# Chunked and channel attention on one core: values ahead of mask and scores on TensorE, low half ahead of the maximum on VectorE

## The reference, cut to what matters

```
scores = einsum('bnqhd,bnkhd->bnhqk', qh, kh) * scale
scores = scores + where(km > 0, 0.0, NEG)
attn = softmax(scores, axis=-1)
out = einsum('bnhqk,bnkhd->bnqhd', attn, vh).reshape(N, T, C)
out = (out @ W_out.T + b_out).transpose(0, 2, 1) * masks + x_of_layer_0
```

## Time and profile before

| what | value |
|---|---|
| median of 3 runs | 1578.93 us (1578.62 to 1580.92) |
| profiled execution | 1581.6 us, span 1579.8 us |
| busy: PE, PEld, DVE, ACT, POOL | 98%, 83%, 85%, 63%, 29% |
| mean granted TensorE clock | 0.991 of full speed |
| period of a sample, from the start of L803 in sample 8 to that in sample 9 | 822.36 to 918.01 us |

### The profile page before, as it was taken

One profiled execution on the slowest core, in us unless ns is written; L12 is line 12 of the kernel. 1 busy time (PEld: TensorE's weight loads), 2 busy tenths in 40 slices (PEclk: granted clock), 3 DMA queues, 4 the chain that ended last, 5 costly groups with the idle time before them and its releaser, 6 DMA issues.

```text
span 1579.8 us, 53821 instructions
## 1 busy us (share of the span) xinstructions
PE 1541.7 (98%) x23816; PEld 1307.8 (83%) x23816; DVE 1339.2 (85%) x2024; ACT 993.3 (63%) x1796; POOL 463.2 (29%) x292
## 2 busy tenths in 40 slices
PE   7999999999999999999999999999999999999994
PEld 6888888888888888888888888888888888888873
DVE  4778889898898888989888898888988889898886
ACT  5557665666656667576576656666566675765753
POOL 0114233142331414124142331423314142241422
PEclk9999999999999999999999999999999999999996
DMA  6132341423323242241523314233242423415021
GB/s 233 60 95 88 96 127 43 148 82 115 109 74 123 69 142 82 94 128 43 150 87 103 122 42 148 82 116 107 68 129 69 141 82 95 128 43 153 31 74 62
DMA packets 96328, 157.22 MB, mean 100 GB/s; under 512 B 5344, under 2 KB 38240, under 8 KB 95968
## 3 DMA queue, kind: packets, MB, share of 16 engines
q1 hardware_dynamic: 96096, 153.78, 31.2%
HBM read 120.20 MB, written 33.55 MB: 97 GB/s over the span
## 4 chain that ended last, share of the span: by engine, by line
PE 97%; DVE 1%; ACT 1%; issue 0%; DMA 0%; POOL 0%; DVEq 0%; SPq 0%; POOLq 0%; ACTq 0%
PE pj_ps L283 46%; PE l_ps L283 12%; PE w_ps L318 7%; PE s_ps L307 7%; PE l_ps L392 7%; PE w_ps L336 6%; PE s_ps L296 3%; PE l_ps L410 2%; PE l_ps L430 2%; PE l_ps L418 1%; PE l_ps L424 1%; PE l_ps L412 1%; PE l_ps L433 1%; DMA y_raw<-in_ctx 0%; PE l_ps L400 0%
## 5 line engine op out<-in xcount | busy, mean ns | idle before, releaser
L946 POOL TENSOR_TENSOR prob<-prob,row_inv 128x1024 f32<-128x1024 f32 x128 | 262.3, 2049 | 927.1 <-DVE row_inv L740 927.1
L596 ACT CAST att_hi<-w_ps 128x256 fp32r<-128x256 f32 x256 | 82.8, 376 | 249.5 <-PE w_ps L336 243.7
L283 PE MATMUL pj_ps<-y_hi,w_hi 128*128 128x512 f32 x512 | 209.0, 408 | 9.3 <-DVE y_lo L705 9.3
L283 PE MATMUL pj_ps<-y_lo,w_hi 128*128 128x512 f32 x512 | 203.3, 397 | 0.0
L283 PE MATMUL pj_ps<-y_hi,w_lo 128*128 128x512 f32 x512 | 203.2, 397 | 0.0
L735 DVE TENSOR_REDUCE row_sum<-prob 128x16 f32<-128x1024 f32 x128 | 155.0, 1211 | 52.3 <-ACT prob L578 52.3
L723 DVE TENSOR_REDUCE row_max<-s_ps 128x16 f32<-128x1024 f32 x128 | 155.9, 1218 | 20.1 <-PE s_ps L307 17.6
L963 POOL TENSOR_TENSOR o_sb<-o_sb,u_sb 128x1024 f32<-128x1024 f32 x63 | 164.7, 2625 | 6.7 <-ACT o_sb L586 6.7
L573 ACT COPY prob_t<-w_ps 128x512 f32<-128x512 f32 x256 | 149.9, 586 | 19.7 <-PE w_ps L318 16.8
L709 DVE TENSOR_TENSOR yt_hl<-yt_raw,yt_hl 128x1024 fp32r<-128x1024 f32 x64 | 119.7, 1870 | 43.0 <-ACT yt_hl L545 41.0
L730 DVE TENSOR_TENSOR prob<-s_ps,row_max 128x1024 f32<-128x1024 f32 x128 | 155.5, 1215 | 0.1
(11 more groups left out here) (110 smaller groups left out, 3581.9 us busy)
## 6 DMA issues: line engine op xcount, KB each, us to landing
y_raw<-in_ctx SPq DMA_DIRECT2D x64, 512.0 KB, 4.9
yt_raw<-in_ctx_t SPq DMA_DIRECT2D x64, 512.0 KB, 4.7
x_raw<-in_x SPq DMA_DIRECT2D x64, 512.0 KB, 5.1
out_z<-o_sb SPq DMA_DIRECT2D x64, 512.0 KB, 3.6
mask_b<-in_mask SPq DMA_DIRECT2D x64, 256.0 KB, 4.0
u_sb<-in_w SPq DMA_DIRECT2D x2, 512.0 KB, 5.0
w_sb<-in_w SPq DMA_DIRECT2D x1, 1024.0 KB, 10.7
cst<-in_consts SPq DMA_DIRECT2D x1, 512.0 KB, 6.9
```

Of the source, the lines that this page charges most:

```text
L283: last = mm(dst, lhs, rhs, start=i == 0, stop=i == len(todo) - 1)
L946: nc.gpsimd.tensor_tensor(cut, cut, row_inv[:, u % 2, :].unsqueeze(2).to_broadcast([P, 2 * HEADS, CHUNK]), ALU.mult).then_inc(probs_done, 1)
```

## The change

On PE, in each even step, the 32 matmuls of `values` move from behind the mask and the scores to ahead of them. Their wait (`values_ready`) stood ahead of the scores already. On DVE, in each even step, the two subtractions of `att_low` move from behind `top` to ahead of it, with their wait for `att_hi_done`. Nothing is added or taken away, and what stands ahead of and behind these three things is as it was. The work behind the last step is not touched.

```
                     if e == 0:
                         if not (first and u < LAG):
                             values_ready(n, u - LAG)
+                            values(n, u - LAG)
                         scores(n, u)
-                        if not (first and u < LAG):
-                            values(n, u - LAG)
...
                     if e == 0:
-                        top(n, u)
                         if not (first and u < LAG):
                             att_low(n, u - LAG)
+                        top(n, u)
                         if s == 0 and not first:
                             group_deviation(n - 1)
                         shift(n, u)
```

## The result

The changed kernel takes 1592.61 us (median of 4 runs, 1589.19 to 1594.30) against 1579.56 (4 runs, 1578.62 to 1580.92): ratio 1.0079, 95% interval 1.0060 to 1.0099. The profiled execution took 1594.3 us, its span is 1592.5. The change makes the kernel 13 us slower.

A forecast was written before the change was run, and what follows sets the result against it. PE, busy 98% of the span, was taken to bound the kernel. 15 samples x 0.86 = 12.9, less 0.3, plus 0.1, gave +12.7 us: median 1591.6, own range 1588 to 1596, wider range 1579.5 to 1606 (0.81).

The forecast's parts named there:

- The hidden wait: PE's transposes in steps 6 and 10 wait 0.15 us for `att_lo`; removing it wins 32 x 0.15 = 4.8 us.
- The seams: PE's switches between kinds of matmul: taken as 0, with bounds of -10 to +10 us over 126 steps.
- The rival of the seams: PE's matmul switches at their bounds, with the main effect: 1581.6 or 1601.6 us; chance 0.09.
- Step 6: Transposes win 0.15 us; DVE's shift comes 0.7 us late, covered by the copy L803, which ends with POOL's join.
- The rival that the copy takes 2.02 us anywhere: L803 on DVE ends 0.7 us late, making step 10's shift 1.6 late: 24 us, time 1603; chance 0.12.
- Step 10: Transposes win 0.15 us; DVE waits for `att_hi` with `top` queued, so the shift is 0.86 us late, and `o_bias` too.
- The wait: PE waits 1.16 us for `o_bias` ahead of `layer0_output` in step 12, in 15 samples.
- The size: Net loss of 0.86 us a sample (bounds 0.74 to 1.01), in 15 samples: 12.9 us.
- no slack at all between step 10 and step 12: DVE, busy 10.58 of 10.68 us up to `o_bias`, passes any delay of step 10's shift on to PE.
- The sum: Whole kernel: 12.9 - 0.3 (first sample) + 0.1 (very end) = +12.7 us, median to 1591.6.
- The clock: A 1.16 us wait lowers TensorE's clock, 1.7 us more in 15 samples: time 1617; chance 0.07.
- The faster case: Early `att_hi` in step 10, or slack up to `o_bias`, leaves only the 4.8 us gains: 1574.1; chance 0.12.

The follow-up runs named there:

- the whole hold gone: Changed kernel with all of `split_y` (ACT's rounding of ctx) moved behind `copy_att` of the next step: 1576.23 us, ratio 0.9980 to the kernel before.
- all but step 10: Kernel before with the new order on PE and DVE in every even step except step 10, which keeps the old: 1579.33 us, ratio 0.9994.
- PE's half: Kernel before with only PE's order changed (values ahead of mask and scores), DVE still taking the maximum first: 1594.71 us, ratio 1.0098.

## Why the prediction was right, point by point

**What bounds.** The hidden wait of 0.15 us in steps 6 and 10 was real and went in both (PE takes 0.18 and 0.19 us less from step 6 to step 8 and from step 10 to step 12); with a repair the change gains, by the medians 2.9 us with `split_y` moved, 4.0 with the scaling moved and 5.3 with both, against 4.8 forecast.

**The seams.** 0 was taken. Values behind projection 0.32, mask behind values 0.79 from start to start, as the projection stood before. The rival of the seams falls.

**Step 6.** The low half was forecast 0.42 us sooner than needed and came 0.43 sooner (it ends at 825.91, the transposes start at 826.48 and need 0.14). The copy was forecast to end 0.15 behind POOL's join; measured 0.16. The rival that the copy takes 2.02 us anywhere falls. The Trainium skill's rule of the locked port pair (SBUF — State Buffer, Who interferes with whom) agrees: the copy started later, took 1.13 us, and ended with the join again.

**Step 10.** The shift was forecast to end 1.01 late against the step's start, measured 1.01 (5.73 against 4.72). The prediction says that the scores are ready 0.8 us sooner; ahead of the maximum it is 1.14 by its own rows, measured 1.13; no term of the sum uses it. The overlap lost between maximum and shift is in the rows: the shift starts 0.04 behind the maximum's end (847.23 + 1.21 = 848.44, 848.48). The Trainium skill's statement that a semaphore between two DVE instructions costs nothing extra (VectorE: DVE Perf Modes, The DRAIN you can't avoid), which it makes of a row of equal copies, does not hold for this pair: 0.04 behind the end, where instructions that don't wait for the one just ahead start 0.08 ahead of its end.

**The wait.** 1.16 us forecast, 1.16 measured.

**The size.** Forecast +0.86 a sample, measured +0.79: the two gains are 0.18 and 0.19 us, not 0.15, the part from step 12 to step 14 is 1.18 longer, and that behind it 0.03 shorter. The term that was mis-sized is the count: 14 samples, not 15. In the last sample ACT rounds nothing in step 9, and I carried the middle sample's row over. The rows of it after, step 10:

```profile
1523.60 0.65 ACT L595 CAST att_hi<-w_ps 128x256 fp32r<-128x256 f32 x2
...
1524.28 0.76 DVE L746 TENSOR_TENSOR att_lo<-w_ps,att_hi 128x256 fp32r<-128x256 f32 x2 [1.08 <-ACT att_hi L595]
...
1529.19 0.75 DVE L751 SCALAR_TENSOR_TENSOR u_sb<-pj_ps,c,mask_b 128x512 f32<-128x512 f32 x1 [0.85 <-PE pj_ps L283]
...
1537.03 0.47 PE L283 MATMUL l_ps<-x_hi,m_hi 128*128 128x512 f32 x1
```

`att_hi` comes 1 us sooner and no wait is marked in step 12, while DVE has 0.85 us to spare in step 11. This is no clean control for the hold, though. The low half of ctx (L704, 1.21 us in sample 8) is missing on DVE too, and before the change DVE was idle there for 1.03 us ahead of the same instruction, enough to swallow a shift that comes 1.01 late. So the prediction's "no slack at all between step 10 and step 12" holds for the middle samples only. The constant 0.26 us behind `o_bias` in sample 15 says that `o_bias` releases PE (2.08 us behind the start of step 12, where 2.06 is the least), but not that a later shift would delay it: DVE itself waits for PE on the way. The proof of the middle samples is the wait itself, and its going when the scaling moved.

**The sum.** From the start of sample 1 to that of sample 15 there are 14 periods, 0.79 us longer each: +11.1. The part ahead of sample 1 is 0.7 shorter and that from the start of sample 15 to the end 0.3, with the two gains of the first and of the last sample in them. That is +10.1, where the forecast had 12.7. The rest was not forecast: some samples are longer than the median, mostly those with the stops told of in the last section, by 5.0 us in all after and by 2.4 before, +2.6. (The idle time marked at the stops is 3.4 and 1.6 us; they cost more than that: before, the sample with the stop of 0.69 us is 0.9 longer than the median.) Together these are the 12.7 us between the spans. So the total was met partly by luck: one sample too many stood for stops I had not foreseen.

**The rivals.** The clock: granted 0.991 after as before. The stretch behind the wait in sample 8 (columns as the earlier trace rows) was granted 1.00, so 1.16 us of idle time did not lower it.

```profile
859.50:863.00 3.50, 3.50 (x15) 2.91 (x16) 3.42 (x5) 1.16 (x2) 0.00 (x0) 1.00 0.77 212
```

The faster case failed at the point it was said to turn on, a shift less than 0.3 late in step 10; with the whole hold gone it came true.

## What to carry to other kernels

When two instructions of an in-order engine change places, ask which engine releases the new first one and what that engine does just before: here the low half was moved up to meet values that came 1.27 us sooner, but the engine between them was busy and passed on 0.25 of that, while the maximum waited behind. Then follow the delayed result along its engine's list to the next place where the bounding engine reads it, and look for idle time on the way. A reordering that gains 5 us can cost 13 until the one long list behind it gets its slack; and to move an optional piece of work behind the needed one gave it at no cost.

## What the runs showed of the hardware that was not expected

**Stops of PE.** In every trace but that of `split_y` moved in the kernel before, PE stops once to five times, nearly always in the middle of the small matmuls, for 0.2 to 1.4 us, with no releaser but its own issue: 1.6 us in all before, 3.4 after, 2.9 with all but step 10, 0.7 with the scaling late. With the order of before it comes in the values (L336), with the changed order in the scores (L307), so it goes with the last block of small matmuls of a step and not with an operation. Between profiles it comes partly in other samples and partly at the same place: at the 35th of the 64 scores near 137.9 us in the trace after and in that of PE's half. No run was made on its cause, but the traces point to one. The DMA queue q8, of the kind "instruction", moves 16 KB at a time, 188 transfers in the execution before. The transfer and the stop near 639 us of the kernel before:

```profile
q8 instruction: 1, 0.02, 1.9%
...
639.64 0.32 PE L336 MATMUL w_ps<-prob_t,v_s 64*32 64x64 f32 x10 [0.69 <-issue]
```

It is the only transfer between 636.9 and 640 us; it lasts from 637.39 to 638.32, and PE goes on 1.32 us behind its end. All 33 stops of this kind in the 12 traces (idle times ahead of `layer0_output` are not of it) end 1.2 to 1.7 us behind the end of such a transfer, a position in which PE is for 5 to 6% of the time. So PE seems to have waited for its own instructions to be loaded. Why most of the transfers go by without a stop is open.

**The spread between executions.** It is not mainly these stops. The 61 executions of the kernel before that ran beside the experiments lie between 1575.4 and 1581.6 us, and the time goes with the mean granted clock: 1580.3 us on average for the 18 at 0.991, 1576.1 for the 7 at 0.995. That is larger than the 2.6 us expected of the run with all but step 10. In the traces, one of each kernel, the difference lies in the last sample, where the clock falls to its lower level for a while: from that sample's first matmul of step 0 to the end, the three executions granted 0.993 or 0.994 took 122.1 to 122.5 us and the six at 0.991 124.2 to 125.2. Two of the three have `split_y` moved, so the clock is not the only difference between them.
